# Two-expert FFN in a macaron block on eight cores: both mask rows kept, masked inputs built in pieces between the second product's additions, and two gates issued later

## The reference

```python
x = x + 0.5 * ffn(layernorm(x))
x = x + attn(layernorm(x))
x = x + 0.5 * ffn(layernorm(x))

def ffn(xf):
    top1 = argmax(softmax(xf @ gate_w.T))            # 2 experts, hard routing
    masked = xf[None] * one_hot(top1).T[:, :, None]  # rows of the other expert become zero
    h = relu(einsum('end,edh->enh', masked, w1) + b1)
    routing = (einsum('enh,ehd->end', h, w2) + b2).sum(axis=0)
    shared = relu(xf @ sw1 + sb1) @ sw2 + sb2
    return routing + shared
```

## Time and profile before

| what | us |
| --- | --- |
| median of 2 timed runs | 5043.79 (4903.68 and 5183.91) |
| the profiled execution's own time | 4949.96 |
| its span on the slowest core (core 1) | 4948.4 |
| spans of the other cores | 4896.2 to 4945.9 |
| TensorE busy on core 1 | 3979.3 |
| VectorE busy | 1354.2 |
| ScalarE busy | 1257.3 |

### The profile page before, as it was taken

The page is one execution under the profiler, slowest core; times in us unless marked ns, Lnnn a source line. Parts: engine busy times, 40 slices in busy tenths (PEclk is TensorE's granted clock), DMA queues, the critical chain, the costliest instruction groups (busy, mean ns, idle before and its releaser), DMA issues. The chain is left out here.

```text
span 4948.4 us, 46427 instructions; the slowest of 8 cores (4896.2 to 4948.4 us)
## 1 busy us (share of the span) xinstructions
PE 3979.3 (80%) x16776; PEld 1614.8 (33%) x16776; DVE 1354.2 (27%) x2551; ACT 1257.3 (25%) x2945; POOL 48.4 (1%) x66
## 2 busy tenths in 40 slices
PE   2569999999888862788887777655999999988888
PEld 0123444444333320222332222222344444433333
DVE  2341112222333335112121111234111222233332
ACT  1101111121111110455536555310111112111111
POOL 0000000000000000000000000000000000000000
PEclk9788999999999975655575565677889999999987
DMA  6002222222122100100001000300222222222201
GB/s 136 0 0 35 35 35 35 35 42 37 25 35 34 18 1 0 17 1 1 1 1 18 1 1 1 52 0 0 34 35 34 35 35 35 35 35 34 35 1 68
DMA packets 55276, 124.69 MB, mean 25 GB/s; under 512 B 1808, under 2 KB 1808, under 8 KB 53008
## 3 DMA queue, kind: packets, MB, share of 16 engines
q0 software_dynamic: 52144, 104.86, 13.8%
q1 hardware_dynamic: 2912, 16.85, 1.0%
HBM read 218.18 MB, written 8.39 MB: 46 GB/s over the span
## 5 line engine op out<-in xcount | busy, mean ns | idle before, releaser
L576 PE MATMUL ps_c<-ar_h,ar_w 128*128 128x512 bf16 x3072 | 808.0, 411 | 322.3 <-DVE x_sb L596 149.7
L555 ACT ACTIVATE ar_h<-ps_a,b1hf 128x512 bf16<-128x512 f32 x384 | 263.9, 687 | 2338.0 <-PE ps_a L545 2338.0
L576 PE MATMUL ps_d<-ar_h,ar_w 128*128 128x512 bf16 x3072 | 768.9, 396 | 0.0
L716 PE MATMUL s<-ar_h 64*128 64x512 bf16 x1024 | 553.9, 566 | 176.3 <-ACT ar_w L727 82.6
L576 PEld LDWEIGHTS ps_c<-ar_h,ar_w 128*128 128x128 bf16 x3072 | 307.8, 103 | 773.1 <-issue 514.3
L545 PE MATMUL ps_a<-ar_b,ar_w 128*128 128x512 bf16 x2048 | 491.3, 383 | 7.3 <-DVE ar_b L511 7.3
L545 PE MATMUL ps_b<-ar_b,ar_w 128*128 128x512 bf16 x2048 | 492.1, 384 | 0.0
L596 DVE TENSOR_TENSOR x_sb<-x_sb,ps_c 128x512 f32<-128x512 f32 x352 | 241.9, 687 | 808.3 <-PE ps_c L576 807.1
L576 PEld LDWEIGHTS ps_d<-ar_h,ar_w 128*128 128x128 bf16 x3072 | 312.9, 102 | 405.5 <-issue 113.8
L727 ACT ACTIVATE ar_w<-s 128x512 bf16<-128x512 f32 x512 | 301.6, 594 | 321.4 <-PE s L716 318.0
L555 ACT ACTIVATE ar_h<-ps_b,b1hf 128x512 bf16<-128x512 f32 x384 | 263.9, 687 | 427.2 <-PE ps_b L545 427.2
(11 more groups left out here) (162 smaller groups left out, 2429.0 us busy)
## 6 DMA issues: line engine op xcount, KB each, us to landing
ar_w<-w1c POOLq DMA_DIRECT2D x24, 2048.0 KB, 18.2
ar_w<-w2c POOLq DMA_DIRECT2D x24, 2048.0 KB, 28.9
x_sb<-x SPq DMA_DIRECT2D x1, 8192.0 KB, 38.2
y<-x_sb SPq DMA_DIRECT2D x8, 1024.0 KB, 8.6
ar_w<-wqt POOLq DMA_DIRECT2D x1, 2048.0 KB, 16.2
ar_w<-wut POOLq DMA_DIRECT2D x1, 2048.0 KB, 17.2
b1hf<-b1h SPq DMA_DIRECT2D x1, 48.0 KB, 39.6
bq_sb<-bqc SPq DMA_DIRECT2D x1, 4.0 KB, 41.1
```

The source lines that it names most:

```text
L555: s.activation(ar_h[:, _hc * TS:(_hc + 1) * TS], _pst[:, :], AF.Relu, bias=b1hf[:, _sup * 8 + _hc:_sup * 8 + _hc + 1], scale=0.5).then_inc ...
L576: ins = t.matmul(_pst[:, :], w2blk(_slot, _hc, _dc), ar_h[:, _hc * TS:(_hc + 1) * TS], start=(_hc == 0), stop=(_hc == NKC - 1))
L716: t.matmul(_sr[:, :], qq_ap(_pa, _h), ar_h[_h:_h + 64, _q4 * TS:(_q4 + 1) * TS], start=True, stop=True).then_inc(S[MM], 1)
```

## The change

It has three parts.

1. **A second mask.** The gate also computes the opposite comparison (`m1row`), spreads it with a second matmul into the other bank, and copies it into `mask_ap(1, st)`. Building for klass 2 becomes one product per chunk, as for klass 1. The copy of a mask waits for all layernorm work, since the place of mask 1 is in use until then.
2. **Pieces.** `build_lnm` is split into 8 pieces, one per chunk. `do_mm1` only puts them on a list; `do_mm2` emits one piece after each of its 8 additions.
3. **Gates later.** In super 0 the gates of strips 0 and 1 are emitted after the `do_mm2` of strips 2 and 3, and those of strips 2 and 3 right behind, so that three gates stand in a row at the end of the super.

```diff
+        m1row = sb("m1row", [1, TS], BF16)
...
-                def fmrow(v, S, _r1=r1, _r2=r2):
+                base_mr = sch.val(DVE)
+                def fmrow(v, S, _r1=r1, _r2=r2, _b=base_mr):
                     v.tensor_tensor(m0row[:, :], _r1, _r2,
                                     ALU.is_ge).then_inc(S[DVE], 1)
+                    v.wait_ge(S[DVE], _b + 1)
+                    v.tensor_tensor(m1row[:, :], _r1, _r2,
+                                    ALU.is_lt).then_inc(S[DVE], 1)
...
                     t.matmul(_bp, onesLb[:, :], m0row[:, :],
                              start=True, stop=True).then_inc(S[MM], 1)
+                    t.matmul(_bp2, onesLb[:, :], m1row[:, :],
+                             start=True, stop=True).then_inc(S[MM], 1)
...
+                sch.wait("vector", DVE, ext.get("all_ln", 0))
...
                     v.tensor_copy(mask_ap(0, _st), _bp).then_inc(S[DVE], 1)
+                    v.wait_ge(S[DVE], _b + 1)
+                    v.tensor_copy(mask_ap(1, _st), _bp2).then_inc(S[DVE], 1)
...
-            def build_lnm(st, klass, wait_mm):
-                tok = 0
-                for kc in range(NKC):
+            pending_lnm = []
+            def build_lnm_pieces(st, klass, wait_mm):
+                which = 0 if klass == 1 else 1
+                def piece(kc):
                     sch.wait("vector", DVE, max(ln_tok[st], mask_tok[st]))
                     sch.wait("vector", MM, wait_mm)
-                    if klass == 1:
...
-                            v.tensor_mul(xb_s[:, :], ln_ap(_kc, _st * TS, TS),
-                                         mask_ap(0, _st)).then_inc(S[DVE], 1)
-                            v.wait_ge(S[DVE], _b + 1)
-                            v.tensor_sub(lnm_ap(_kc), ln_ap(_kc, _st * TS, TS),
-                                         xb_s[:, :]).then_inc(S[DVE], 1)
...
+                    def fm(v, S, _kc=kc, _st=st, _w=which):
+                        v.tensor_mul(lnm_ap(_kc), ln_ap(_kc, _st * TS, TS),
+                                     mask_ap(_w, _st)).then_inc(S[DVE], 1)
+                    sch.emit("vector", fm)
+                    lnm_tok[0] = sch.bump(DVE, 1)
+                return [lambda _kc=kc: piece(_kc) for kc in range(NKC)]
...
-                    lnm_tok[0] = build_lnm(nst, nkl, prev_mm1[0]) if nkl else None
+                    if nkl:
+                        pending_lnm.extend(build_lnm_pieces(nst, nkl, prev_mm1[0]))
+                    else:
+                        lnm_tok[0] = None
...
                     ps2_free[dc % 2] = stt_tok[dc][st]
+                    if pending_lnm:
+                        pending_lnm.pop(0)()
+                while pending_lnm:
+                    pending_lnm.pop(0)()
...
                 do_mm2(0, st, 0, sch.val(DVE))
                 ext["bc_wait"] = sch.val(DVE)
+                if st == 2:
+                    ext["all_ln"] = max(ln_tok)
+                if st >= 2:
+                    gf[st - 2]()
+            for st in (2, 3):
+                ext["bc_wait"] = sch.val(DVE)
                 gf[st]()
```

More of the change, by code:

```diff
@@ L457, in stage_gate, with fmb, fmbe @@
                 sch.wait("vector", DVE, gevac)
-                def fmrow(v, S, _r1=r1, _r2=r2):
+                base_mr = sch.val(DVE)
+                def fmrow(v, S, _r1=r1, _r2=r2, _b=base_mr):
                     v.tensor_tensor(m0row[:, :], _r1, _r2,
                                     ALU.is_ge).then_inc(S[DVE], 1)
+                    v.wait_ge(S[DVE], _b + 1)
+                    v.tensor_tensor(m1row[:, :], _r1, _r2,
+                                    ALU.is_lt).then_inc(S[DVE], 1)
                 sch.emit("vector", fmrow)
-                mrow_tok = sch.bump(DVE, 1)
+                mrow_tok = sch.bump(DVE, 2)
                 sch.wait("tensor", DVE, mrow_tok)
-                def fmb(t, S, _bp=bA):
+                bB2 = bcps[1]
+                def fmb(t, S, _bp=bA, _bp2=bB2):
                     t.matmul(_bp, onesLb[:, :], m0row[:, :],
                              start=True, stop=True).then_inc(S[MM], 1)
+                    t.matmul(_bp2, onesLb[:, :], m1row[:, :],
+                             start=True, stop=True).then_inc(S[MM], 1)
                 sch.emit("tensor", fmb)
-                mbt = sch.bump(MM, 1)
+                mbt = sch.bump(MM, 2)
                 sch.wait("vector", MM, mbt)
-                def fmbe(v, S, _st=st, _bp=bA):
+                sch.wait("vector", DVE, ext.get("all_ln", 0))
+                base_me = sch.val(DVE)
+                def fmbe(v, S, _st=st, _bp=bA, _bp2=bB2, _b=base_me):
                     v.tensor_copy(mask_ap(0, _st), _bp).then_inc(S[DVE], 1)
+                    v.wait_ge(S[DVE], _b + 1)
+                    v.tensor_copy(mask_ap(1, _st), _bp2).then_inc(S[DVE], 1)
                 sch.emit("vector", fmbe)
-                mask_tok[st] = sch.bump(DVE, 1)
+                mask_tok[st] = sch.bump(DVE, 2)
             stats_fns = [lambda _st=st: stage_stats(_st) for st in range(NSTRIP)]
@@ L502, in emit_ffn, with build_lnm @@
             lnm_tok = [None]
-            def build_lnm(st, klass, wait_mm):
-                tok = 0
-                for kc in range(NKC):
+            pending_lnm = []
+            def build_lnm_pieces(st, klass, wait_mm):
+                which = 0 if klass == 1 else 1
+                def piece(kc):
                     sch.wait("vector", DVE, max(ln_tok[st], mask_tok[st]))
                     sch.wait("vector", MM, wait_mm)
-                    if klass == 1:
-                        def fm(v, S, _kc=kc, _st=st):
-                            v.tensor_mul(lnm_ap(_kc), ln_ap(_kc, _st * TS, TS),
-                                         mask_ap(0, _st)).then_inc(S[DVE], 1)
[L513 to L518, removed]
-                            v.tensor_mul(xb_s[:, :], ln_ap(_kc, _st * TS, TS),
-                                         mask_ap(0, _st)).then_inc(S[DVE], 1)
-                            v.wait_ge(S[DVE], _b + 1)
-                            v.tensor_sub(lnm_ap(_kc), ln_ap(_kc, _st * TS, TS),
-                                         xb_s[:, :]).then_inc(S[DVE], 1)
-                        sch.emit("vector", fm)
-                        tok = sch.bump(DVE, 2)
-                return tok
+                    def fm(v, S, _kc=kc, _st=st, _w=which):
[4 more added lines that the diff above has]
+                return [lambda _kc=kc: piece(_kc) for kc in range(NKC)]
+            def build_lnm(st, klass, wait_mm):
+                for p in build_lnm_pieces(st, klass, wait_mm):
+                    p()
+                return lnm_tok[0]
             def do_mm1(sup, st, klass, slot):
@@ L608, in emit_ffn @@
                     pf[st + 1]()
+                if st + 1 == NSTRIP:
+                    pass
                 do_mm2(0, st, 0, sch.val(DVE))
+                ext["bc_wait"] = sch.val(DVE)
[4 more added lines that the diff above has]
+            for st in (2, 3):
                 ext["bc_wait"] = sch.val(DVE)
```

## The result

The changed kernel is faster: the ratio to the kernel before is 0.970, with a 95% interval of 0.964 to 0.975. The lowest timed execution is 4763.06 us against 4903.68. The ratios here leave out the executions in which a die stayed at a clock of 0.81 for a large part of the time; the medians over all executions contain them, 5012.18 us (12) against 5150.3 us (10). The forecast had the direction and, on a core that is never at 0.81, the size; but 5012 lies outside its range of 4770 to 4960 us, because the range was built around 4949.96 us as the level of before and ten executions of that kernel have a median of 5150.3.

A forecast was written before the change was run, and what follows sets the result against it. TensorE's work plus its pauses was taken to bound the kernel. Klass 2's stall (-223.9), the new wait (+89.3) and super 0 (+24.3) gave -110.3 us from 4949.96, about 4840 us, range 4770 to 4960.

The forecast's parts named there:

- Klass 2's stall goes, 223.9 us: Second product in klass 2 strips: no more waiting for VectorE's addition or half clock behind it, 223.9 us less.
- The new wait, 62 x 1.44: Each strip's first product waits for the eighth piece behind the last addition: 62 times 1.44 us, 89.3 us more.
- Super 0, 24.3 us: Gates in super 0: second comparison and matmul 8.1, mask-copy waits 2.6, half clock 13.6, together 24.3 us more.
- Sum, -110.3 us: Whole kernel: -223.9 + 89.3 + 24.3 = -110.3 us, ending at about 4840 us.
- The base: Level of the kernel before from which the sum was subtracted: the profiled execution, 4949.96 us.
- Rival 1: New waits at strip starts also cost clock, 62 x 2.4 = 149 us, ending at 4989 us; chance 0.10 in part or full.
- Rival 2: Denser klass 2 is held at clock 0.81, 173 us more, ending at 5013 us; chance 0.12.
- Rival 3: In klass 2 only the wait of 149.7 us goes and half clock stays, ending at 4914 us; chance 0.03.
- Rival 4: Super 0's row of gates keeps its clock with short hand-overs, 4823 us; chance 0.75 together with the main forecast.

The follow-up runs named there:

- changed_again: The changed kernel itself, unaltered, run once more beside the kernel before on the same chip; ratio to before 0.967 (0.961-0.973).
- extra_rest: The kernel before with the gate of strip 3 done three times at the end of super 0; ratio to before 1.000 (0.999-1.001).
- pause_sweep: The changed kernel with 0 to 7 extra idle products ahead of the last piece, more in later supers; pauses 1.3 to 3.7 us, no whole-kernel time given.
- gates_late: The kernel before with only the change's later order of gates, one mask and the old build in one block; ratio to before 0.988 (0.979-0.997).
- six_ahead: The kernel before with mask 1 as 1 - mask 0, last relu awaited only before the eighth matmul, late gates, six build products ahead of additions; ratio 0.927.
- gates_in_place: The changed kernel with mask 1 in a free part of another tile and each gate behind its strip as before; ratio to before 0.969 (0.964-0.974).

## Why the prediction was right and wrong

- *Klass 2's stall goes, 223.9 us.* Right. Klass 2 strips became as long as those of klass 1 at a clock of 1.00, wait and half clock together. Either way out is enough alone: the pieces without the second mask (pieces_two_ops) and the second mask without the pieces (whole_build).
- *The new wait, 62 x 1.44.* Right: 1.43 us, 62 times, and whole_build gives 95 us back.
- *Super 0, 24.3 us.* Right on an undisturbed core. Super 0 and the strip behind it, FFN 1 and FFN 2, before (cores 6 and 4) and in changed_again (core 0), columns as in the earlier trace rows:

```profile
118.16:408.63 290.47, 190.87 (x738) 0.81 0.10 14
3234.88:3526.17 291.29, 193.16 (x752) 0.79 0.10 15
```

```profile
117.97:418.05 300.08, 195.98 (x743) 0.79 0.09 14
3151.27:3455.19 303.92, 199.64 (x742) 0.77 0.09 14
```

That is 9.6 and 12.6 us, 22 together. But the row of gates did something that this step never asked: it was costed as a loss alone, and it makes the stretches at 0.81 rarer. Over all kernels of the table but extra_rest, pairs with stretches are 95 of 150 with gates in place and 21 of 128 with late gates. Pairs more than 75 us above the lowest did not become rarer: 54 of 204 and 60 of 188.

- *Sum, -110.3 us.* The undisturbed times give -112. The measured ratio of 0.970 is a larger gain than the 0.978 of the forecast, and the difference (some 35 us) is the slowest core: it had one or two stretches before and mostly one after (4781 to 4787 us against 4758 undisturbed).
- *The base.* This is the step that failed. "From the profiled execution: 4949.96 - 110.3" took one execution for the level of all. The two timed runs stood 280 us apart, which I wrote down and did not use: the range was built from 4949.96 and from the lower run, and the same sum from the upper one, 5183.91 - 110.3 = 5074, lies outside it. The median of 10 runs of before is 5150.3, 200 us above the base that I took; 5150.3 x 0.970 = 4996 and 5150.3 - 110.3 = 5040, either side of the 5012 measured. The unit of such a forecast is the ratio, and its range in us has to span the executions of before.
- *Rival 1* fell by the sweep. *Rival 2* was wrong as a rule of klass 2: FFN 1 was at 1.00 on core 0. As an event it occurred, FFN 2 of the same core was at 0.81; but gates_late shows the same with the stalls in place, and six of the ten executions of before are above 5140 us, so no run shows that the denser klass 2 brings it. The Trainium skill ("TensorE: Matmul & The Clock Gate", Part 1) has 0.81 last as long as the dense load; six_ahead, the densest kernel here, had a profiled execution in which none of the eight cores was at 0.81 at any time (spans 4545.9 to 4553.5 us, the windows above at 1.00). *Rival 3* fell: strips of klass 2 are as long as those of klass 1, 30.15 us. *Rival 4* was the wrong way round: super 0 cost 22 of its 24 us, and the late gates gave back more elsewhere.

## What to carry to other kernels

Work on a buffer for the next step, put ahead of an engine's drains of PSUM, costs nothing as long as it fits into the time until the first bank is needed, and spreading it to the last drain moves it onto the critical path; put it as early as the bank allows (here six chunks ahead, two behind), and look again whenever a pause that hid it goes. On eight cores compare undisturbed cores first: they show a change of 10 us where medians of whole executions differ by hundreds. Then ask separately whether the change alters how often cores are granted less clock.

## What the runs showed of the hardware

- A pause of TensorE costs clock by chance, and shorter ones than the 4.74 us of the stall do: none of 492 pauses of 1.28 us (changed_again), none of 64 of 1.5 us, 37 of 256 of 2.00 us (pieces_two_ops), 16 of 64 of 2.1 to 2.3 us, 27 of 64 of 2.2 to 2.6 us, 41 of 64 of 2.8 to 3.1 us, all of 64 of 3.3 us or more (pause_sweep, supers 6 to 10, eight cores). Each time the half clock lasted 3.4 us, which costs 1.7 us.
- The clock of 0.81 comes in stretches, often of 160 us, for pairs of cores, mostly in super 0 or at the start of dense work. With the late order, a row of three gates of some 30 us before the dense work, they were rarer: 21 of 128 pairs of cores over five kernels with late gates, 95 of 150 over five with gates in place (of these gates_in_place, with its longer gates, had only 4 of 14). Why is not shown.
